# Count table of a graph network: one half of the groups stays on VectorE, the other goes over ScalarE and GpSimd

## The reference, cut to what matters

```python
def _fast_rgcn_layer(x, src, tgt, edge_type, W_r, root_r, bias_r):
    seg = tgt * R + edge_type
    agg = segment_sum(x[src], seg, N * R).reshape(N, R, d)
    cnt = segment_sum(ones, seg, N * R).reshape(N, R, 1)
    agg = agg / clip(cnt, 1.0, None)
    return einsum('nrd,rdo->no', agg, W_r) + x @ root_r + bias_r
```

## Time and profile before

| what | value |
|---|---|
| median of 3 runs | 3430.39 us |
| profiled execution | 3430.7 us |
| its span | 3428.9 us |
| the counting stage, by the trace | 101.4 to 179.4 us |
| VectorE busy in the whole span | 2191.1 us, 64% |
| GpSimd busy in the whole span | 1220.1 us, 36% |

### The profile page before, as it was taken

How to read it: one execution, slowest core, us unless ns; L and a number is a source line. 1 busy time by engine, 2 the same in 40 slices (tenths; PEclk the granted TensorE clock), 3 DMA queues, 4 the chain that set the end, 5 groups by cost and what they waited for, 6 DMA issues and landing times.

```text
span 3428.9 us, 80954 instructions
## 1 busy us (share of the span) xinstructions
PE 2657.8 (78%) x24551; PEld 1772.1 (52%) x24552; DVE 2191.1 (64%) x7930; ACT 1322.9 (39%) x2936; POOL 1220.1 (36%) x1269
## 2 busy tenths in 40 slices
PE   3337777768899994888888878888888788888887
PEld 1323333335556683555555555556555555555555
DVE  6689999976454463655566656566666556656565
ACT  0149999963222212333333333333333333333332
POOL 3020000000000002555555535555555455555554
PEclk9569999999999997999999999999999999999999
DMA  0011111121110026444444444444444444444443
GB/s 25 20 57 46 44 44 46 43 65 47 32 45 23 10 78 182 115 120 122 122 121 120 120 112 123 122 122 117 122 121 127 124 113 120 122 121 121 121 122 82
DMA packets 240377, 313.35 MB, mean 91 GB/s; under 512 B 41585, under 2 KB 213724, under 8 KB 240268
## 3 DMA queue, kind: packets, MB, share of 16 engines
q1 hardware_dynamic: 199596, 225.59, 24.9%
q0 software_dynamic: 40672, 86.39, 8.6%
HBM read 268.23 MB, written 43.59 MB: 91 GB/s over the span
## 4 chain that ended last, share of the span: by engine, by line
PE 24%; DMA 15%; issue 10%; DVE 4%; another core or an unknown queue 3%; POOL 3%; ACT 1%; DVEq 0%; SPq 0%; POOLq 0%; ACTq 0%
DMA arena<-pair,arena 15%; PE psum L2289 7%; PE psum L2302 7%; PE psum L2313 4%; PE psum L2266 3%; POOL arena L2206 3%; DVE arena L2478 2%; DVE arena L2474 1%; PE psum L2279 1%; DVE arena L2484 1%; PE psum L2240 0%; DVE arena L2514 0%; PE psum L2247 0%; DMA arena<-in_gbase 0%
## 5 line engine op out<-in xcount | busy, mean ns | idle before, releaser
L2206 POOL DMA_INDIRECT arena<-pair,arena x1212 | 1161.8, 959 | 936.8 <-DMA h<-h 360.4
L2484 DVE SCALAR_TENSOR_TENSOR arena<-psum,arena,work 128x304 f32<-128x304 f32 x606 | 427.7, 707 | 701.3 <-DMA h<-h 437.5
L2302 PE MATMUL psum<-arena 128*128 128x304 f16 x3939 | 571.1, 294 | 27.1 <-issue 23.9
L2420 ACT ACTIVATE arena<-psum 128x512 f16<-128x512 f32 x303 | 180.7, 596 | 1037.9 <-remote 757.1
L2289 PE MATMUL psum<-arena 128*128 128x304 f16 x2424 | 370.4, 296 | 207.2 <-DMA arena<-pair,arena 150.0
L2478 DVE TENSOR_SCALAR arena<-arena 128x304 f16<-128x304 f16 x2121 | 482.8, 299 | 0.0
L2302 PEld LDWEIGHTS psum<-arena 128*128 128x128 f16 x3939 | 361.5, 98 | 207.0 <-issue 92.3
L2266 PE MATMUL psum<-arena 128*32 128x256 f16 x7272 | 361.4, 278 | 120.9 <-issue 109.4
L2417 ACT ACTIVATE arena<-psum 128x1024 f16<-128x1024 f32 x303 | 309.3, 1021 | 321.8 <-DMA h<-h 173.6
L2289 PEld LDWEIGHTS psum<-arena 128*128 128x128 f16 x2424 | 213.3, 98 | 346.2 <-issue 246.0
L2313 PE MATMUL psum<-arena 128*128 128x152 f32 (+1 forms) x2496 | 376.8, 296 | 6.4 <-DVE arena L2484 5.8
(11 more groups left out here) (288 smaller groups left out, 3224.4 us busy)
## 6 DMA issues: line engine op xcount, KB each, us to landing
work<-inverse SPq DMA_DIRECT2D x606, 152.0 KB
arena<-pull SPq DMA_DIRECT2D x303, 224.0 KB
pull<-rows SPq DMA_DIRECT2D x101, 224.0 KB
arena<-pair,arena POOLq DMA_INDIRECT x1212
h<-work SPq DMA_DIRECT2D x8, 640.0 KB
h<-h POOLq DMA_DIRECT2D x8, 640.0 KB, 6.9
pair<-arena SPq DMA_DIRECT2D x12, 256.0 KB
x_pad<-arena SPq DMA_DIRECT2D x1, 1600.0 KB, 7.2
```

The source lines that it names most:

```text
L2206: e.indirect_dma_start(out=t.msg[:, j, k].rearrange("p h f -> p (h f)"), out_offset=None, in_=d[f"pair_{l}"].rearrange("n h f -> n (h f)") ...
L2302: m = e.matmul(p.psum[:, 1, 0:KEYS], t.smsg[:, j % 2, tile, half, :], t.soh[:, j % 2, tile, :], start=(tile == 0 and half == 0), stop=(til ...
L2484: e.scalar_tensor_tensor(t.agg[h % 2][:, :, k % BATCH, :], p.psum[:, k % 2, 0:KEYS].rearrange("p (r w) -> p r w", r=REL), t.back[:, l:l + ...
```

## The change

Groups q = 2 and 3 of each round leave VectorE. ScalarE waits until TensorE has finished the six rounds of a bank, and copies the counts of quarter 2 and of quarter 3 out of it as fp16 into a new field `t.copies`: two instructions a bank, 18 in all. GpSimd adds them into the table, 100 additions, each of one group. It reads the bases with its own loads and registers. Its additions wait for ScalarE's copy (once for each quarter and bank) and for the addition two before them. VectorE keeps q = 0 and 1, 102 additions, and its own wait is now for the addition two before. Both fill 12 registers with each load, every second pair of bases, so that a load now serves 6 rounds. TensorE's wait before it uses bank 0 again asks for both readers.

```diff
+    def load(e, regs, part, q):
+        first, stop = part * 2 * LOAD, min(GPAD, (part + 1) * 2 * LOAD)
+        if first < NG:
+            e.load(regs[part % 2][0:(stop - first) // 2],
+                   t.gbase[0:1, first:stop].rearrange("p (m g) -> p m g", g=G)[:, :, q:q + 2])
     @block.gpsimd
         e.memset(t.x[:, BLOCKS - 1, :], 0.0).then_inc(s_tail, 1)
+        e.wait_ge(s_tail, 1)
+        regs = [[e.alloc_register(f"copy_base{q}_{k}") for k in range(LOAD)] for q in range(2)]
+        load(e, regs, 0, 2)
+        done = 0
+        for n in range(NG):
+            if n % (2 * LOAD) == 0:
+                load(e, regs, n // (2 * LOAD) + 1, 2)
+            m, q = n // G, n % G
+            if q < 2:
+                continue
+            base = e.snap(regs[n // (2 * LOAD) % 2][n % (2 * LOAD) // G * 2 + q - 2], min_val=0, max_val=NODES - 1)
+            to = t.quarters[32 * q:32 * q + REL, bass.ds(base, RWIN)]
+            if m % PER_BANK == 0:
+                e.wait_ge(s_cp, 2 * (m // PER_BANK) + q - 1)
+            if done > 1:
+                e.wait_ge(s_ag, done - 1)
+            e.tensor_tensor(to, to, t.copies[32 * q:32 * q + REL, m * RWIN:(m + 1) * RWIN], ALU.add).then_inc(s_ag, 1)
+            done += 1
     @block.vector
+        done = 0
         for n in range(NG):
-            if n % LOAD == 0 and n + LOAD < NG:
-                more = min(LOAD, NG - n - LOAD)
-                e.load(regs[n // LOAD % 2 ^ 1][0:more], t.gbase[0:1, n + LOAD:n + LOAD + more])
+            if n % (2 * LOAD) == 0:
+                load(e, regs, n // (2 * LOAD) + 1, 0)
             m, q = n // G, n % G
+            if q > 1:
+                continue
...
-            if n >= G:
-                e.wait_ge(s_ad, n - G + 1)
+            if done > 1:
+                e.wait_ge(s_ad, done - 1)
...
     @block.scalar
...
+        for h in range(BANKS):
+            m0, m1 = h * PER_BANK, min(NG // G, (h + 1) * PER_BANK)
+            e.wait_ge(s_mm, m1)
+            for q in (2, 3):
+                sums = p.psum[32 * q:32 * q + REL, h % 8, 0:(m1 - m0) * WIDE].rearrange("p (m w) -> p m w", w=WIDE)
+                e.activation(t.copies[32 * q:32 * q + REL, m0 * RWIN:m1 * RWIN].rearrange("p (m w) -> p m w", w=RWIN),
+                             sums[:, :, q * RWIN:(q + 1) * RWIN], ACT.Copy).then_inc(s_cp, 1)
     @block.tensor
...
             if m >= 8 * PER_BANK:
-                e.wait_ge(s_ad, PER_BANK * G)
+                e.wait_ge(s_ad, PER_BANK * 2)
+                e.wait_ge(s_cp, 2)
```

More of the change, by code:

```diff
@@ L457, in count_relations @@
     whole = (BLOCKS - 1) * P
+    BANKS = -(-ROUNDS // PER_BANK)
     s_16, s_hot, s_rest, s_mm, s_ad, s_tail, s_x = (p.sem(n) for n in (
         "halves", "hot", "rest", "counted", "added", "tail", "x"))
+    s_cp, s_ag = p.sem("copied"), p.sem("added_of_copies")
     block = Bodies()
@@ L487, in _ @@
         typ, dloc = (a.rearrange("p (g n) -> p g n", g=G) for a in (t.typ16, t.dloc16))
-        e.load(regs[0], t.gbase[0:1, 0:LOAD])
+        load(e, regs, 0, 0)
         e.wait_ge(s_16, 2)
@@ L495, in _ @@
             one.then_inc(s_hot, 1)
+        done = 0
         for n in range(NG):
-            if n % LOAD == 0 and n + LOAD < NG:
-                more = min(LOAD, NG - n - LOAD)
-                e.load(regs[n // LOAD % 2 ^ 1][0:more], t.gbase[0:1, n + LOAD:n + LOAD + more])
+            if n % (2 * LOAD) == 0:
+                load(e, regs, n // (2 * LOAD) + 1, 0)
             m, q = n // G, n % G
+            if q > 1:
+                continue
             bank, at = place(m)
-            base = e.snap(regs[n // LOAD % 2][n % LOAD], min_val=0, max_val=NODES - 1)
+            base = e.snap(regs[n // (2 * LOAD) % 2][n % (2 * LOAD) // G * 2 + q], min_val=0, max_val=NODES - 1)
             to = t.quarters[32 * q:32 * q + REL, bass.ds(base, RWIN)]
@@ L2570, in outside @@
     t.typ16, t.dloc16 = (p.work[:, GPAD + NPAD + k * TPAD // 2:GPAD + NPAD + (k + 1) * TPAD // 2].bitcast(F16) for k in range(2))
+    t.copies = p.work[:, GPAD + NPAD + TPAD:GPAD + NPAD + TPAD + 25 * RWIN].bitcast(F16)
 def edge_columns(p):
```

## The result

The changed kernel takes 3419.55 us in the median of 10 runs (3415.03 to 3424.09), the kernel before 3431.19 (3428.3 to 3441.07): a ratio of 0.9963, 95% interval 0.9953 to 0.9973. That is 11.6 us faster. The forecast was 3400, some 30 us less. The time lies inside the range of 3397 to 3428, but that range took in several mechanisms, and the one behind the 3400 did not come out. The profiled execution took 3415.03 us, its span is 3413.3.

What follows compares the result with a forecast made beforehand. VectorE's additions were taken to bound the counting stage, read by itself up to its barrier; halving them saves 30.6 us, 0.3 comes back, so 3430.7 - 30.3 = 3400.4, given as 3400 us, range 3397 to 3428.

Steps and rivals of the forecast that it cites:

- the one behind the 3400: Counting stage: VectorE sets the end, at 146.9 against 177.5 us; 3400 us, own range 3397 to 3404, chance 0.50.
- the loads: Between sets of additions: a strided load of 12 registers takes 0.848 us, at most 1.1 more a load.
- The two loads that I put ahead of the additions: Start of the counting stage: VectorE's two first loads come before its additions, as one did behind the fields; costed at nothing.
- loads longer than 0.85: Sign in the changed profile: the prediction is wrong if the register loads take longer than 0.85 us.
- The barrier and the norm stage move with the end: After the counting stage: norm's first instruction at 149 in place of 179.5 us, every later stage shifted alike.
- GpSimd's price: Counting stage: GpSimd's 100 additions start 0.23 us apart, ending at 143, under VectorE's 146.9 while below 0.27.
- The half select plus wait: GpSimd's additions: select 0.29 plus wait 0.16 is 0.45 a turn; waiting for the addition two before gives P = 0.23.
- The whole select: GpSimd's additions: P = 0.29, line 247's select, would end the stage at 149.1, taking 2 us of the gain back.
- the rival in which GpSimd sets the end: Counting stage: GpSimd ends last but the kernel gains; P = 0.4 gives 3413, band 3402 to 3423, chance 0.23.
- The lock rival: Counting stage: VectorE's and GpSimd's additions lock each other out and alternate, 0.37 us a pair; end 159.2, 3412, chance 0.05.
- 0.3 was allowed for all of them: Start of GpSimd's additions: 0.3 us back for up to six that start while VectorE still writes its fields.
- TensorE no bound: Counting stage: TensorE makes a bank in 3.4 us, VectorE takes 3.89, so it never catches up; TensorE ends at 138.3.

Runs made afterwards that it cites:

- aligned kernel: Changed kernel plus copies putting each engine's bases side by side, both halves beginning at a multiple of 4 words: 3178.38 us against 3197.96 for the kernel before, ratio 0.9935.
- plain: Changed kernel with the old loads, 12 neighbouring bases for three rounds, 17 loads on each engine: 3188.24 us, ratio 0.9954 to the kernel before.

## Why the prediction was wrong

- **The step that failed: the loads.** "I take 0.848, the row for twelve registers", with an upper bound of 1.9 us. Measured 2.80. The bound took one separate read for every pair; measured is one for every register, 0.09 + 12 x 0.22 = 2.7. Inside the additions there are six full loads and one of six registers: 6 x 1.95 + 0.9 = 12.6 us. The two loads that I put ahead of the additions weren't free either: one makes VectorE's fields start 1.03 us late, the other the additions 0.94. Together 14.6 of the 15.9 us by which VectorE ended later than forecast (162.4, against 146.9 less the 0.4 by which this execution's stage began earlier). The rest are pauses of 0.41 to 0.47 us within three sets, where the forecast had a step's 0.12 (0.9 together), and a first set 0.25 longer. The aligned kernel removes the price of the loads, at the cost of two copies, 0.40 us together, and its counting stage is 27.2 us shorter than before (77.9 to 50.7), where 30.6 was forecast: VectorE ends 2.7 later than forecast, GpSimd 1.1 behind it, and 0.4 comes back at the barrier. Line 891, 4 registers for 0.346, would have hinted that neighbours come in fours, and line 2341 that from a wrong word they don't. The prediction did name loads longer than 0.85 as a sign of being wrong.
- **What I cost at nothing: the next stage.** "The barrier and the norm stage move with the end" was false by 7.0 us. 4.6 of it is the lock, which nothing in the change touches: norm is 36.0 with it and 31.3 without it, with the late branch in neither. The late branch is 3.6 us late on its own (4.1 against 0.54), but it costs the stage 2.4, from 38.3 to 35.9, since SyncE would have ended it a little later than VectorE anyway. I had seen the lock in the earlier trace rows and looked for it only in the counting stage.
- **GpSimd's price, near miss.** P, the time from start to start of its additions, is 0.293, forecast 0.23, with 0.27 as the point where GpSimd sets the end. With long loads it ends together with VectorE (162.5 and 162.4), in the aligned kernel 1.1 us behind. The half select plus wait that gave 0.23 was the wrong sum: waits cost nothing here, the change of the first partition does. The whole select, 0.29, has the right size, though nothing shows that it has the same cause. The measured 3420 lies in the band of the rival in which GpSimd sets the end with P from 0.28 to 0.5. That is luck: with this P alone the forecast's own sum gives some 28 us of gain, and what took the gain was no term of that rival.
- **The lock rival, in the counting stage.** VectorE's additions took 0.166 us beside GpSimd's, 0.171 alone: no lock between them. By the rule of the Trainium skill, "SBUF — State Buffer", Who interferes with whom, that the prediction quotes, a VectorE instruction with at most one SBUF input, outside the 2-port modes, does not contend with GpSimd, and the 0.166 agrees. But GpSimd's first addition, two SBUF operands beside VectorE's last fields, took 1.76 us, where 0.3 was allowed for all of them.
- **Right:** 102 additions in sets of 2.88 (2.90 forecast), gap 0.99 with a good load, 18 copies of 0.26 on ScalarE, TensorE no bound, its granted clock 0.50 in the whole stage as before.
- **Against the median.** The counting stage gained 15.0, norm gave back 7.0, and the adjacency stage gained 1.8: 9.8 us, within the interval of 9.3 to 16.1 that the ratio gives. In the two profiled executions the relational layers begin 10.9 us earlier (1290.5 against 1301.4), near the 11.6 of the medians. The 4.7 beyond that in the spans are not a gain that the medians show: the profiled execution of the changed kernel is the lowest of its ten.

## What to carry to other kernels

Price an instruction of the sequencer by its size and address as one does a transfer: list every row of its kind with its count before bounding it. Here an edit that halved the number of loads and broke up their runs of four neighbours lost more than it saved (62.8 us for the stage, against 55.7 in `plain`). And behind a stage that gets shorter, look at what two engines do beside each other in the next one; how long one is kept out is not carried over from the old trace.

## What I had not expected of the hardware

- A load of registers took 0.09 us and 0.25 for each four neighbours from a word that is a multiple of 4 (4: 0.346, 8: 0.60, 12: 0.85, 24: 1.62), and 0.22 for each register otherwise (6: 1.40, 12: 2.72 neighbours and 2.80 as pairs). Six from a good word took 0.83, one four and two single ones. Words one or two off were alike.
- GpSimd's additions of 19 columns: 0.18 us from start to start on one first partition, 0.29 where it changes or where each waits for the last (tried on partitions 64 and 96 in turn); 16, 64 or 128 partitions made no difference.
- A VectorE instruction over 25 columns was kept out for 8.46 us by GpSimd's clears, 11 of them 1.37 apart; with 0.06 between them it got in after 0.68. Why in the kernel before it slipped in between two of them is open: it arrived 1.24 us into a clear there, and in the changed kernel too.
- From a taken branch to the next instruction VectorE needed 0.2, 0.6, 2.8, 3.7 or 4.1 us, depending on the code that lay ahead of it, run or not. Which distance is a good one was not tried.
